# Hybrid attention and Mamba block: half the rows go ahead through projection, conv and dt, and z and the second half's dt are made inside the scan

## The reference

```
x = x + attention(layernorm(x))                 # 16 heads of 16, rotary, causal
x = x + ffn(layernorm(x))                       # both factors rounded to a 6-bit grid, blocks of 32
x = x + b(layernorm(x))
x = x + ffn(layernorm(x))

b(u):  v  = u + mamba(rmsnorm(u))
       return v + silu(rmsnorm(v) @ w1.T) @ w2.T

mamba(v): xp, z = split(v @ in_proj.T)          # 512 columns each
          xc = silu(causal conv of 4 taps over xp + conv_b)
          x_dbl = xc @ x_proj.T                 # 16 for dt, 16 for B, 16 for C
          dt = softplus(x_dbl[:16] @ dt_proj.T + dt_b)
          h[t] = h[t-1] * exp(dt*A) + dt*xc*B   # 512 channels x 16 states
          y = sum over states of h*C, + xc*D
          return (y * silu(z)) @ out_proj.T
```

## Time and profile before

| | |
|---|---|
| median of 3 runs | 10043.31 us (10042.93 to 10044.33) |
| the profiled execution's own time | 10042.81 us |
| its span | 10040.9 us, 98208 instructions |
| DVE busy | 7696.5 us, 77% |
| ACT, POOL busy | 4309.5 us, 4340.3 us (43% each) |
| mean granted PE clock | 0.898 |

### The profile page before, as it was taken

One profiled execution on the slowest core, in us unless ns is written; L12 is line 12 of the kernel. 1 busy time (PEld: TensorE's weight loads), 2 busy tenths in 40 slices (PEclk: granted clock), 3 DMA queues, 4 the chain that ended last, 5 costly groups with the idle time before them and its releaser, 6 DMA issues. The chain is left out here.

```text
span 10040.9 us, 98208 instructions
## 1 busy us (share of the span) xinstructions
PE 7867.1 (78%) x31796; PEld 3819.5 (38%) x31796; DVE 7696.5 (77%) x11686; ACT 4309.5 (43%) x8247; POOL 4340.3 (43%) x2663
## 2 busy tenths in 40 slices
PE   5787787787877878787887878778787787877877
PEld 2343343433434334343343433434343343432434
DVE  4787877779687686876868768787787877878777
ACT  2534535354442543525435254353534535345352
POOL 1451714518154171542716336262361724517145
PEclk8898988989889898888989889898898988989889
DMA  3010020200202002020020200102011020100202
GB/s 76 1 38 15 5 48 1 51 1 5 48 0 51 1 9 44 0 51 1 12 40 0 51 1 21 32 0 52 1 28 25 0 52 1 38 15 5 48 0 51
DMA packets 260295, 229.91 MB, mean 23 GB/s; under 512 B 22051, under 2 KB 232739, under 8 KB 259635
## 3 DMA queue, kind: packets, MB, share of 16 engines
q1 hardware_dynamic: 259782, 223.48, 11.6%
HBM read 151.60 MB, written 70.25 MB: 22 GB/s over the span
## 5 line engine op out<-in xcount | busy, mean ns | idle before, releaser
L625 POOL TENSOR_TENSOR arena<-arena 128x1024 f32<-128x1024 f32 x1024 | 2434.3, 2387 | 1330.6 <-DVE arena L1007 879.0
L766 ACT ACTIVATE PS<-arena,Aneg 128x512 f32<-128x512 f32 x2048 | 1410.6, 691 | 1627.2 <-DVE XNT L1047 883.2
L690 ACT ACTIVATE arena<-PS 128x512 f32<-128x512 f32 (+3 forms) x3072 | 1286.8, 509 | 867.0 <-PE PS L1213 861.8
L914 DVE TENSOR_REDUCE pm<-PS 128x1 f32<-128x512 f32 (+3 forms) x1728 | 1050.6, 661 | 336.5 <-PE PS L1192 234.9
L1327 PE MATMUL PS<-XNT,identf 128*128 128x512 f32 x2048 | 1012.1, 618 | 320.0 <-POOL XNT L608 320.0
L587 POOL TENSOR_SCALAR_AFFINE_SELECT arena<-arena 128x512 f32<-128x512 f32 x512 | 328.2, 641 | 2114.5 <-ACT arena L690 2114.5
L1189 PE MATMUL PS<-arena 96*128 96x512 bf16 (+3 forms) x3072 | 1098.0, 382 | 178.8 <-PEq L1411 87.3
L1327 PE MATMUL PS<-arena,identf 128*128 128x512 f32 x2048 | 1025.5, 624 | 161.8 <-DVE arena L1023 161.8
L1213 PE MATMUL PS<-arena 99*128 99x512 bf16 (+3 forms) x3072 | 891.8, 331 | 5.4
L1150 PE MATMUL PS<-identf,arena 128*128 128x128 f32 x1280 | 284.1, 387 | 776.0 <-POOL arena L577 664.6
L1312 PE MATMUL PS<-arena,sel 96*128 96x512 bf16 x1664 | 513.4, 391 | 389.2 <-DVE arena L1023 319.7
(11 more groups left out here) (140 smaller groups left out, 13240.7 us busy)
## 6 DMA issues: line engine op xcount, KB each, us to landing
pieces_scratch<-arena SPq DMA_DIRECT2D x816, 64.0 KB
arena<-pieces_scratch SPq DMA_DIRECT2D x34, 768.0 KB
arena<-pieces_scratch SPq DMA_DIRECT2D x51, 512.0 KB
arena<-pieces_scratch SPq DMA_DIRECT2D x17, 1536.0 KB
arena<-in_x SPq DMA_DIRECT2D x17, 1024.0 KB, 5.6
U<-in_x SPq DMA_DIRECT2D x17, 1024.0 KB, 5.6
arena<-pieces_scratch SPq DMA_DIRECT2D x17, 1024.0 KB
out<-X SPq DMA_DIRECT2D x64, 256.0 KB, 8.3
```

Source lines behind the costliest of these rows:

```text
L625: nc.gpsimd.tensor_tensor(DB[:, n % 2], DTU[:, j, half(th)].unsqueeze(1).to_broadcast([P, SP2, TH]), BB[:, SP2 * sg:SP2 * (sg + 1), :], AL ...
L690: A(PT[s % len(PT)][:, hh, 0:w], bank(t_bank(n))[:, 0:w], ACT.Exp, scale=DH ** -0.5)\
L766: A(bank(da_bank(m)), DT[:, j, half(th)], ACT.Exp, scale=Aneg[:, j, SP2 * sg + ss:SP2 * sg + ss + 1]).then_inc(S("dA"), 1)
L914: V_.tensor_reduce(out=dst, in_=bank(r % 3)[:, 0:share * w].rearrange("p (h w) -> p h w", h=share), op=ALU.max, axis=AX.X, negate=True).th ...
```

## The change

The scratch layout changes so that halves can overlap: the first quantization's tiles move up by 8208 columns, `sel` keeps one column per state and is read with a stride of 0, two h buffers leave `XNT` for an own buffer `HS2`, `DTR` and `BR` have one half, and `TZ` (one buffer instead of two) shares `BR`'s place.

The rms norm of the Mamba part is folded into the layer norm: a second small DVE step makes `vr`, POOL's `joint_power` its power, and `joint_rows` writes the doubly normed rows straight from X. The squares on ACT and four POOL steps go. `U` is still written.

Silu of the conv is ACT's own Silu, in place, for half a tile; the DVE product goes. All conv work is by halves: 8 units of 512 columns instead of 4 of 1024.

```diff
-            def tanh_c(m):
-                act.wait_ge(S("convd"), m + 1)
-                A(TC[:, m, :], XC[:, m, :], ACT.Tanh).then_inc(S("tc"), 1)
+            def conv_0(n):
+                th, j = divmod(n, ND)
+                at = DC - 1 + th * TH
+                act.wait_ge(S("ip"), n + 1)
+                A(XP[:, j, at:at + TH], bank(xp_bank(n)), ACT.Copy).then_inc(S("xp"), 1)
+                act.wait_ge(S("xp"), n + 1)
+                A(XC[:, j, half(th)], XP[:, j, at:at + TH], ACT.Identity, scale=convw[:, j, DC - 1:DC],
+                  bias=convb[:, j:j + 1]).then_inc(S("conv0"), 1)
+            def silu_c(n):
+                th, j = divmod(n, ND)
+                act.wait_ge(S("convd"), n + 1)
+                A(XC[:, j, half(th)], XC[:, j, half(th)], ACT.Silu).then_inc(S("xc"), 1)
```

The order on DVE. The second half's quantization pauses after its eighth step for the first half's residual tiles:

```diff
+            for ins in quantize(own, 2 * C, [...SECOND], pause=True):
+                if ins is None:
+                    dve.wait_ge(S("xb"), 1)
+                    add_tiles(1, X, range(NT)[tiles(0)])
+                else:
+                    ins.then_inc(S("q"), 1)
+            joint_rows(0)
+            own.did(V_.memset(XP[:, :, 0:DC - 1], 0.0))
+            layer_norm(1, 0, lambda i: U[:, i, :])
+            conv(0)
+            conv(1)
+            dve.wait_ge(S("xb"), NTH)
+            add_tiles(1, X, range(NT)[tiles(1)])
+            joint_rows(1)
+            conv(2)
+            conv(3)
+            layer_norm(1, 1, lambda i: U[:, i, :])
+            conv(4)
+            conv(5)
+            split_bc(0)
+            conv(6)
+            conv(7)
+            for n in range(ND):
+                relu_dt(n, n)
...
             times_u(0)
+            split_bc(1)
```

On PE and on ACT, between the first quantized products and the scan (calls joined to fewer lines here):

```diff
+            turn_joint(FIRST); in_proj(0); in_proj(1); quant_products(0, 1)      # PE
+            in_proj(2); in_proj(3); turn_joint(SECOND)
+            x_proj(0, 0); x_proj(0, 1); in_proj(4); x_proj(0, 2); in_proj(5); x_proj(0, 3)
+            in_proj(6); in_proj(7); dt_proj(0, 0); dt_proj(1, 1)
+            pe.wait_ge(S("bc"), 1)
+            spread_b(0)
+            pe.wait_ge(S("xp"), ND * NTH)
+            dt_proj(2, 2); dt_proj(3, 3); spread_b(1)
+            for j in range(ND):
+                x_proj(1, j)
+            pe.wait_ge(S("drl"), ND)
...
+            conv_0(0); conv_0(1); evacuate(1, SECOND); conv_0(2); conv_0(3)      # ACT
+            silu_c(0); silu_c(1); evacuate(2, SECOND); silu_c(2); conv_0(4); silu_c(3); conv_0(5)
+            split_bc(0); conv_0(6); conv_0(7); silu_c(4); silu_c(5); abs_dt(0, 0); silu_c(6)
+            abs_dt(1, 1); silu_c(7); abs_dt(2, 2); abs_dt(3, 3)
+            exp_dt(0)
+            ln_dt(0, slice(0, 1))
+            ln_dt(0, slice(1, ND))
             spread_b(0)
+            split_bc(1)
```

Inside the scan twelve side steps are placed, z tiles and the second half's dt tiles, and one Ln of the whole second half. Before its side products PE waits until DVE has read the same bank (two side steps earlier); ACT's Tanh waits for DVE's product of the z before:

```diff
+        SIDE = [("z", 0)] + [("dt", k) for k in range(ND)] + [("z", k) for k in range(1, 2 * ND)]
+        SIDE_AT = dict(zip((8, 9, 10, 11, 12, 14, 16, 18, 34, 36, 38, 40), SIDE))
+        LN_AT = 20
...
+                    if n in SIDE_AT:                   # PE, ahead of step n's C spread
+                        kind, k = SIDE_AT[n]
...
+                        if kind == "dt":
+                            dt_proj(ND + k, side_bank(n))
+                        else:
+                            project(ND + z_unit(k)[0], z_unit(k)[1], bank(side_bank(n)))
...
+                if n in SIDE_AT:                       # ACT, behind dA(2n), dA(2n+1), B copy
+                    if kind == "dt":
+                        abs_dt(ND + k, side_bank(n))
+                        if k == ND - 1:
+                            exp_dt(1)
+                    else:
+                        act.wait_ge(S("ip"), ND * NTH + k + 1)
...
+                        A(TZ, bank(side_bank(n)), ACT.Tanh).then_inc(S("tz"), 1)
+                if n == LN_AT:
+                    ln_dt(1, slice(0, ND))
...
+                if n - 1 in SIDE_AT:                   # DVE, one step later, behind times_c
+                    if kind == "dt":
+                        relu_dt(ND + k, side_bank(n - 1))
+                    else:
+                        silu_z(k, side_bank(n - 1))
```

More of the change, by code:

```diff
@@ L186, in build @@
         two = [t.rearrange("p (n s t) -> p n s t", n=2, s=SP2)
-               for t in (view(28688, 2 * SP2 * TH), XNT[:, :, :].rearrange("p c t -> p (c t)"))]
+               for t in (view(28688, 2 * SP2 * TH), HS2[:, :])]
         HS = [two[0][:, 0], two[0][:, 1], two[1][:, 0], two[1][:, 1]]
@@ L742, in spread_b, with ln_dt @@
+            def ln_dt(th, js):
+                act.wait_ge(S("dte"), th + 1)
+                A(DT[:, js, half(th)], DT[:, js, half(th)], ACT.Ln, bias=1.0).then_inc(S("dtl"), 1)
             def spread_b(k):
@@ new lines, in turn_joint, with project @@
+            def turn_joint(pairs):
+                turn(2, lambda p, tt: RM[0][2 * p + tt], "R", lambda p: 2 * p + 2, pairs)
+            def project(column, th, out):
+                pe.wait_ge(S("te_done"), turn_no(2, (NT // 4) * (th + 1) - 1) + 1)
+                for c in range(NC):
+                    ins = MM(out, ipw[:, c, column * P:(column + 1) * P], XNT[:, c, half(th)],
+                             start=c == 0, stop=c == NC - 1)
+                ins.then_inc(S("ip"), 1)
+            def in_proj(n):
+                th, j = divmod(n, ND)
+                if n >= 2:
+                    pe.wait_ge(S("xp"), n - 1)
+                project(j, th, bank(xp_bank(n)))
@@ L1262, in tensor_program, with x_proj, dt_proj @@
+            def x_proj(th, j):
+                pe.wait_ge(S("xc"), th * ND + j + 1)
+                MM(bank(4 + th)[0:SR + DR, :], xpw[:, j, :], XC[:, j, half(th)], start=j == 0, stop=j == ND - 1)\
+                    .then_inc(S("xpr"), 1)
+            def dt_proj(n, out):
                 th, j = divmod(n, ND)
                 pe.wait_ge(S("bca"), th + 1)
-                if n == 2:
-                    pe.wait_ge(S("z"), 4)
-                if n >= 6:
-                    pe.wait_ge(S("dab"), n - 5)
-                    pe.wait_ge(S("drl"), n - 5)
@@ L1269, in tensor_program, with selector @@
-                MM(bank(DT_BANK[n]), dtw[:, tile(j)], DTR[0:DR, half(th)], start=True, stop=True)\
-                    .then_inc(S("dtp"), 1)
+                MM(bank(out), dtw[:, tile(j)], DTR[0:DR, :], start=True, stop=True).then_inc(S("dtp"), 1)
+            def selector(s):
+                return sel[:, s:s + 1].to_broadcast([3 * 2 * DS, P])
             def spread_b(k):
@@ L1275, in spread_b @@
                 for ss in range(SP2):
-                    ins = MM(bank(6 + ss), sel[:, SP2 * sg + ss, :], BCP[:, half(th)], start=True, stop=True)
+                    ins = MM(bank(6 + ss), selector(SP2 * sg + ss), BCP[:, half(th)], start=True, stop=True)
                 ins.then_inc(S("Bg"), 1)
-            pe.wait_ge(S("bc"), NTH)
-            pe.wait_ge(S("drl"), ND * NTH)
-            pe.wait_ge(S("dab"), ND * NTH)
-            for k in range(4):
-                if k % 2 == 0:
-                    spread_b(k // 2)
-                in_proj(ND * NTH + 4 + k)
-            pe.wait_ge(S("z"), ND * NTH)
+            turn_joint(FIRST)
+            in_proj(0)
+            in_proj(1)
+            quant_products(0, 1)
+            in_proj(2)
+            in_proj(3)
+            turn_joint(SECOND)
+            x_proj(0, 0)
+            x_proj(0, 1)
+            in_proj(4)
+            x_proj(0, 2)
+            in_proj(5)
+            x_proj(0, 3)
+            in_proj(6)
+            in_proj(7)
+            dt_proj(0, 0)
+            dt_proj(1, 1)
+            pe.wait_ge(S("bc"), 1)
+            spread_b(0)
+            pe.wait_ge(S("xp"), ND * NTH)
+            dt_proj(2, 2)
+            dt_proj(3, 3)
+            spread_b(1)
+            for j in range(ND):
+                x_proj(1, j)
+            pe.wait_ge(S("drl"), ND)
             pe.wait_ge(S("diag"), ND)
```

311 lines of the change are left out of this document (161 added, 150 removed), and 4 rows, old and new, of the table names.

## The result

The changed kernel takes 10,531.6 us (median of four, 10,528.8 to 10,534.1) against 10,043.6 for the kernel before: a ratio of 1.0486 [1.0468, 1.0504], 488 us slower, 30.5 us a pass. Forecast were 10,237 us and a range up to 10,350. The direction was right and the size was not.

What follows compares the result with a forecast made beforehand. No engine full: engines wait on each other before the scan; from step 8 DVE bounds it. Scan +24.1, before it -12: +12.1 us a pass, x16 = +194 on 10,042.81, giving 10,237 us; range 10,050 to 10,350.

Steps and rivals of the forecast that it cites:

- Before the scan: Stretch from second half's quantization to first scan: first scan starts 12 us a pass earlier, bounds 0 and 20.
- DVE's added work: Inside the scan, eight products and four max steps moved onto DVE: 7.5 us a pass.
- Table loads: ACT's function switches: six loads a pass, four more than before, 1.28 us each, work following at once.
- the rival of doubled switches: ACT empties before each table switch, costing as much again as the load: +83 us, 10,320 us; chance 0.03.
- Max steps held by POOL: Rival: four in-scan max steps reading PSUM wait for POOL, 1.2 us each: +77 us, 10,314 us; chance 0.10.
- The stalls: In the scan, DVE waits for dA behind ACT's side functions, which wait for PE's side matmuls: 18.4 us a pass.
- No stalls: Rival: ACT and PE run further ahead, only DVE's 7.5 us is paid in the scan: 9,971 us; chance 0.12.
- The condition given for it: The no-stall case decides once the chain from C product to dA, priced at 5.4 us, falls under 4.0.
- The upper bound of the scan part: Work moved into the scan costs at most 33 us a pass, if each of twelve steps stalls by 2.1.

Runs made afterwards that it cites:

- experiment 5: Changed kernel without PE's side matmuls inside the scan, ACT's and DVE's side instructions kept (z and second half's dt not computed): 9,958.0 us.
- experiments 2, 3 and 6: Changed kernel with eight unused matmuls ahead of eight side steps: 10,372.7 us; with sixteen: 10,428.4 us; with second half's x_proj issued before spread_b(1): 10,362.0 us.
- both: Changed kernel with PE's side matmuls issued one step earlier and the second half's x_proj issued before spread_b(1): 9,893.9 us.
- experiment 11: Changed kernel with side matmuls one step earlier, x_proj before spread_b(1), and the second half's Ln at step 21 instead of 20: 9,867.9 us.
- experiment 4: Changed kernel with z inside the scan projected from the first 128 input columns only, two matmuls instead of four each: 10,420.0 us.

## Why the prediction was right in direction and wrong in size

**Before the scan: right.** Forecast 12 us earlier, measured 11.8 in the mean; single passes lie between 9.4 and 12.9, so that the two agree to 0.2 us is in part luck. The layout holds point by point (less the offset): load for Exp 997.2 forecast and 998.2 measured, second x_proj from 1005.5 and 1006.5, first scan 1014.8 and 1015.15. The x_proj at the low clock behind 11 us of idling is there too (timeline of PE: two selectors, then the eight records of x_proj). They take 5.05 us; seven distances of 0.43 and the last record's 0.6 would be 3.6, so three or four distances are wide where I had five:

```profile
1037.16 1.04 PE L1364 MATMUL PS<-arena,sel 96*128 96x512 bf16 x2 [11.30 <-ACT arena L775]
1037.99 5.05 PE L1348 MATMUL PS<-arena,xpw 128*112 128x512 f32 x8
```

**DVE's added work: right.** Forecast 7.5, measured 7.8 (experiment 5: the stretch is 7.1 longer, with the stall behind Ln and less the waits filled).

**Table loads: right.** Six a pass, and the load starts right behind the ACTIVATE before it and the next one 0.01 us behind the load (timeline of ACT), so nothing besides the load's 1.28 is paid; the rival of doubled switches falls:

```profile
1008.13 0.82 ACT L741 ACTIVATE arena<-arena,convb,convw 128x512 f32<-128x512 f32 x1
1008.97 1.28 ACT L747 ACT_TABLE_LOAD   x1
1010.26 1.15 ACT L747 ACTIVATE arena<-arena 128x512 f32<-128x512 f32 x2
```

**Max steps held by POOL: refuted.** All 128 keep their 743 ns (747 before) and none waits:

```profile
L1054 DVE TENSOR_SCALAR arena<-PS,dtb 128x512 f32<-128x512 f32 x128 | 91.6, 743 | 0.0
```

**The stalls: the step that failed.** "Sum **18.4 us**" was measured as 35.2 (35.9 of idle time before eleven scans, less the 0.70 that stood before scan 9 already). In the prediction every link of the chain was priced at the high clock: "selector pair 0.43, four products 1.75, side matmuls 1.9, tanh 0.51, dA 0.69, hand-offs 0.15: 5.4 us". Here is the chain of step 14 in the trace after. DVE's C product ends at 1109.8; PE, then ACT, then DVE:

```profile
1109.88 1.04 PE L1436 MATMUL PS<-arena,sel 96*128 96x512 bf16 x2 [4.34 <-DVE arena L1106]
1110.71 3.62 PE L1453 MATMUL PS<-arena,identf 128*128 128x512 f32 x4
1114.13 2.82 PE L1336 MATMUL PS<-XNT,ipw 128*128 128x512 f32 x4
```

```profile
1116.98 0.60 ACT L836 ACTIVATE arena<-PS 128x512 f32<-128x512 f32 x1 [8.02 <-PE PS L1336]
1117.47 1.30 ACT L815 ACTIVATE PS<-arena,Aneg 128x512 f32<-128x512 f32 x2
```

```profile
1118.29 2.34 DVE L1130 TENSOR_TENSOR_SCAN HS<-PS,arena 128x512 f32<-128x512 f32 x2 [4.45 <-ACT PS L815]
```

PE had idled 4.34 us. The selectors then take 0.8, the products 3.4 instead of 1.75, the side matmuls 2.8 instead of 1.9: 8.5 us from the C product to the scan (1118.29 - 1109.8) where the forecast had 5.4. Each stall of DVE makes PE wait longer for the next C product, and here PE comes out of that wait at the low clock (1.2 GHz, distances of 0.85; granted clock 0.56, first row of the windows below).

The cleanest view of it is one step at two clocks in the same run. PE and DVE around step 37, once in the second pass, once in the fifth; the order of work is the same, and so is PE's wait just before:

```profile
1202.03 3.78 PE L1453 MATMUL PS<-HS,identf 128*128 128x512 f32 x4 [1.81 <-POOL HS L639]
1205.60 3.16 PE L1336 MATMUL PS<-XNT,ipw 128*128 128x512 f32 x4
...
1210.11 1.28 DVE L1130 TENSOR_TENSOR_SCAN arena<-PS,hlast,arena 128x512 f32<-128x512 f32 x1 [4.93 <-ACT PS L815]
```

```profile
3149.04 1.98 PE L1453 MATMUL PS<-HS,identf 128*128 128x512 f32 x4 [1.80 <-POOL HS L639]
3150.86 1.88 PE L1336 MATMUL PS<-XNT,ipw 128*128 128x512 f32 x4
...
3154.09 1.28 DVE L1130 TENSOR_TENSOR_SCAN arena<-PS,hlast,arena 128x512 f32<-128x512 f32 x1 [1.89 <-ACT PS L815]
```

The granted clock in the chain of step 14, and then over these matmuls in the second and in the fifth pass (windows, as above):

```profile
1109.88:1116.90 7.02, 7.02 (x11) 3.09 (x12) 3.96 (x4) 0.00 (x0) 3.37 (x2) 0.56 0.01 2
1202.00:1208.70 6.70, 6.67 (x9) 2.73 (x10) 3.18 (x3) 0.00 (x0) 4.58 (x2) 0.54 0.00 0
3149.00:3152.70 3.70, 3.66 (x9) 1.63 (x10) 3.19 (x3) 0.00 (x0) 3.70 (x2) 1.00 0.00 0
```

At the high clock the stall is 1.89 us, and the forecast for it was 2.0; at the low clock it is 4.93. Eleven of the fourteen passes have the low clock there. The whole pass is hardly shorter in the other three (648.3 us against 648.6): they take 233.6 us instead of 237.1 from step 8 to the last gate, but reach the first scan 3 us later (79.3 against 76.2 us from the norm).

To split the 35.2 us, I took in each pass the unbroken run of matmuls that ends with the side matmuls, and summed what their distances have over 0.43 us. Beside it stands the shortest stall with high-clock distances, in whichever of the changed kernel and experiments 2, 3 and 6 has one (scan 17's still holds one wide distance):

| before scan | forecast | measured | of it wide distances | shortest at the high clock |
|---|---|---|---|---|
| 9 (less 0.70) | 2.75 | 2.75 | 0 | 2.72 |
| 11 | 0.65 | 2.63 | 1.13 | 1.11 |
| 13 | 0.7 | 1.95 | 0 | 1.95 |
| 15 | 1.3 | 4.10 | 2.22 | 1.43 |
| 17 | 1.1 | 3.57 | 1.55 | 1.91 |
| 19 | 2.1 | 4.03 | 1.52 | 2.34 |
| 21 (Ln) | 1.4 | 1.67 | - | 1.67 |
| 35 | 2.8 | 2.77 | 0 | 2.77 |
| 37 | 2.0 | 4.28 | 2.00 | 1.89 |
| 39 | 1.25 | 3.30 | 1.85 | 1.37 |
| 41 | 2.3 | 4.12 | 1.27 | 2.49 |
| sum | 18.4 | 35.2 | 11.5 | 21.7 |

The surplus is 16.8 us a pass. 11.5 (distances) to 13.5 (35.2 - 21.7) of it is the low clock (the lower number goes by the distances, the upper one by stalls taken from other passes and kernels, where what stands before the stall can differ too); the rest, 3.3 to 5.3, is stepping that was too short even at the high clock, above all at the dt steps (scans 11 and 13) and at scan 17. Experiments bear the split out: with eight idle matmuls the wide distances fall from 11.5 to between 4 and 4.5 (by how wide is counted) and the stalls by 8.3; with half of z's matmuls they stay (11.8) while the remainder falls by 7.7.

From there to the 41.1: DVE +7.8, idle time +33.3 net of the waits filled, forecast 7.5 and 16.6. The forecast of 12.1 us a pass fell short of the measured 30.8 by 18.7; of these 17.0 lie in this stretch, 16.7 of them in idle time. Left out of the forecast and still open are the +2.1 us a pass behind the scan (34 us of the 488); DVE's and PE's work there is unchanged and no experiment was aimed at it; the same stretch takes 135.7 us in "both" and 134.2 in experiment 11, whose work there is the same.

**The rivals.** "No stalls" was the fate of the experiment that issued in time: its 9,971 us lie near the measured 10,006. The condition given for it, the chain under 4.0 us, isn't how it came about: the chain left the path instead. The upper bound of the scan part, 33 (DVE's 7.5 and twelve stalls of 2.1), was too low as well against the 41.1 measured, since its 2.1 came from the same high-clock chain; it gives +21 a pass and 10,380 us, while the eleven measured stalls are 3.2 us each on average. The row that should have moved both was among the rows read: matmuls 0.85 us apart at a granted clock of 0.55. I used that price before the scan, where PE waits, and not in the stalls, where I had just worked out that it would wait too.

## What to carry to other kernels

Work for a third engine that rides in a pipelined loop has to be issued by its producer one step before its consumer reads it; behind an in-order engine a late producer delays everything queued after the reader, here the critical dA (525 us for one index). When you predict stalls, price the matmuls inside them at TensorE's low clock as the other bound, since that engine idles in them too (4.34 us above). And look for what stands behind a waiting instruction without needing its result, like x_proj behind the second spread (170 us by itself, 112 on top of the other edit).

## What the hardware showed that I had not expected

- The granted clock is a matter of the exact course of a pass: at step 37 of one run 11 passes have the wide matmul distances and three don't, a stall of 4.93 against 1.89 us, with identical instructions and the same wait of PE before them (1.81 and 1.80 us). That wait alone doesn't decide it; what does is open.
- Idle matmuls pay (eight in each of eight steps: 159 us less), but more of them don't pay more (sixteen: 56 us worse than eight), although the clock rose from 0.94 to 0.98.
- Removing PE work from the late chain (experiment 4) left the clock at 0.89 and won about its own length only (7.4 us a pass for 6.9 us of matmuls).
